# A fused sandwich layer on one core: y kept in the projection's bank, small operations moved to GpSimd, every engine's order rewritten

## What is computed

```
n   = layernorm(x)
o   = causal_conv(n, K) + D_vec * n          # K[d,t] = C[d] * sigmoid(A[d])**t * B[d], per channel
z   = n + gelu(o) @ W_proj.T + b_proj
y   = layernorm(z) * gamma + beta
t   = x + layernorm(y)
m   = layernorm(t); m_prev = m shifted by one token
r   = sigmoid((mu_r*m + (1-mu_r)*m_prev) @ W_r.T)
k   = relu((mu_k*m + (1-mu_k)*m_prev) @ W_k.T)**2
out = t + layernorm(r * (k @ W_v.T))
```

## Time and profile before

| | before |
|---|---|
| median of three runs | 176.42 us (175.55 to 176.43) |
| the profiled execution | 176.38 us |
| its span, first to last instruction | 174.7 us |
| PE matmul busy | 139.6 us (80% of the span), 913 matmuls |
| DVE busy | 146.9 us (84%), 433 instructions |
| ACT busy | 141.4 us (81%), 423 instructions |
| POOL busy | 130.5 us (75%), 149 instructions |
| mean granted TensorE clock | 0.962 of full speed |

### The profile page before, as it was taken

How to read it: one execution, slowest core, us unless ns; L and a number is a source line. 1 busy time by engine, 2 the same in 40 slices (tenths; PEclk the granted TensorE clock), 3 DMA queues, 4 the chain that set the end, 5 groups by cost and what they waited for, 6 DMA issues and landing times.

```text
span 174.7 us, 3232 instructions
## 1 busy us (share of the span) xinstructions
PE 139.6 (80%) x913; PEld 116.4 (67%) x913; DVE 146.9 (84%) x433; ACT 141.4 (81%) x423; POOL 130.5 (75%) x149
## 2 busy tenths in 40 slices
PE   0177556599997899799899999999998989899600
PEld 0065455599687796697687687987796769577600
DVE  0968899967899999999999999999999999933610
ACT  4456985768879989699799599799969997998960
POOL 4357478406996987576889989965989995897794
PEclk9999999669999999999999999999999999999975
DMA  4699500000000000000000100201100101405115
GB/s 114 161 274 338 165 0 2 4 0 0 0 0 2 4 0 4 0 4 0 0 0 4 60 4 0 64 0 60 60 4 13 49 7 55 126 9 171 60 60 180
DMA packets 18673, 8.98 MB, mean 51 GB/s; under 512 B 1504, under 2 KB 18656, under 8 KB 18656
## 3 DMA queue, kind: packets, MB, share of 16 engines
q1 hardware_dynamic: 18224, 8.79, 17.3%
q10 hardware_dynamic: 432, 0.00, 0.1%
HBM read 4.59 MB, written 4.19 MB: 50 GB/s over the span
## 4 chain that ended last, share of the span: by engine, by line
DVE 50%; PE 30%; issue 7%; POOL 6%; ACT 4%; ACTq 1%; POOLq 1%; DVEq 0%
DVE x_all L450 11%; DVE y L433 7%; DVE y_raw L383 4%; DVE t_raw L383 4%; DVE conv_scaled L418 4%; PE ps_v L634 4%; PE ps_prefix L580 4%; DVE conv L424 4%; PE ps_k L613 3%; PE ps_k L614 3%; DVE f L466 3%; PE ps_r L625 3%; PE ps_r L624 3%; PE ps_z L595 3%; DVE x_raw L383 2%
## 5 line engine op out<-in xcount | busy, mean ns | idle before, releaser
L279 ACT ACTIVATE xn<-x_all,x_bias,x_r 128x128 f32<-128x128 f32 x64 | 25.9, 494 | 3.4 <-POOL x_bias L187 3.0
L335 ACT ACTIVATE f_normal<-f,out_bias,f_r 128x128 f32<-128x128 f32 x64 | 26.2, 488 | 2.7 <-POOL out_bias L235 2.7
L595 PE MATMUL ps_z<-pv_T,gelu 128*128 128x128 f32 x128 | 23.8, 289 | 3.3 <-DVE y L433 1.6
L450 DVE SCALAR_TENSOR_TENSOR x_all<-y,y_r,x_all 128x128 f32<-128x128 f32 x64 | 25.8, 470 | 0.0
L624 PE MATMUL ps_r<-mixed_T,tsT 128*128 128x128 f32 x128 | 24.8, 276 | 0.8 <-ACT tanh L329 0.8
L211 POOL TENSOR_TENSOR y<-y,beta_row 128x512 f32<-128x512 f32 x16 | 20.4, 1275 | 6.4 <-DVE y L433 6.4
L625 PE MATMUL ps_r<-mixed_T,tsT 128*128 128x128 f32 x128 | 24.7, 275 | 0.0
L595 PEld LDWEIGHTS ps_z<-pv_T,gelu 128*128 128x128 f32 x128 | 20.4, 200 | 5.8 <-issue 4.0
L580 PE MATMUL ps_prefix<-prefix_ones,xn_pow 128*128 128x256 f32 x64 | 21.3, 417 | 2.1 <-DVE conv_scaled L418 2.0
L194 POOL TENSOR_TENSOR xn_pow<-xn,pow_token 128x512 f32<-128x512 f32 x16 | 20.4, 1278 | 1.8 <-ACT xn L279 1.8
L307 ACT ACTIVATE t_scaled<-x_all,t_r 128x128 f32<-128x128 f32 x64 | 20.3, 393 | 1.5 <-POOL t_r L223 1.4
(11 more groups left out here) (85 smaller groups left out, 358.7 us busy)
## 6 DMA issues: line engine op xcount, KB each, us to landing
out_x<-x_all SPq DMA_DIRECT2D x16, 256.0 KB, 2.2
x_all<-in_x SPq DMA_DIRECT2D x7, 512.0 KB, 5.9
x_all<-in_x SPq DMA_DIRECT2D x2, 256.0 KB, 3.6
w_pv<-in_W_proj SPq DMA_DIRECT2D x1, 64.0 KB, 4.6
w_pv<-in_W_v SPq DMA_DIRECT2D x1, 64.0 KB, 4.7
w_rk<-in_W_r SPq DMA_DIRECT2D x1, 64.0 KB, 5.0
w_rk<-in_W_k SPq DMA_DIRECT2D x1, 64.0 KB, 3.5
gamma_row<-in_gamma SPq DMA_DIRECT2D x1, 64.0 KB, 3.0
```

Source lines behind the costliest of these rows:

```text
L279: last = a_.activation(tile(xn[u % D], j), xa(u, j), ACT.Identity, bias=col(x_bias, u, j), scale=col(x_r, u, j))
L335: last = a_.activation(tile(f_normal[u % D], j), tile(f[u % D], j), ACT.Identity, bias=col(out_bias, u, j), scale=col(f_r, u, j))
L450: last = v_.scalar_tensor_tensor(xa(u, j), tile(y[u % D], j), col(y_r, u, j), xa(u, j), ALU.mult, ALU.add)
L595: t_.matmul(tile(ps_z[u % 2], j), tile(gelu[u % D], j), pv_T[:, 0, :], start=True, stop=False)
```

## The change

- **y stays in the bank.** `scale_z` and `add_beta` go. A new `gamma_z` [DVE] multiplies the whole bank by gamma in place (one 128x512 instruction, it waits for `square_z`); the new `scale_z` [DVE] does z * z_r + beta in place, four tiles. Statistics and residual read the bank. The SBUF ring `y` is gone. `project(u)` now waits for `residual(u - 2)` in place of `scale_z(u - 2)`.
- **Small operations.** The five 128x4 DVE instructions per unit (L443, L444, L459, L475, L476) go. Variance plus eps is now a POOL `tensor_scalar` ahead of each power, for one unit or a pair; the minus sign of the means is avoided by a negated W_v, a subtraction in out_bias and one in `add_f`. `keep_pv` becomes two instructions.
- **Statistics of x.** `POOLED` is 12: POOL takes the powers for units 4 to 11 too, in four pairs; `x_rsqrt` remains for units 12 to 15.
- **t of odd units.** `scale_t_pool` scales t on POOL for units 1, 3, 5, 7, 9, 11 and 13; ACT keeps the other nine.
- **Orders.** The four lists are rewritten.

```diff
-    POOLED = 4
+    POOLED = 12
+T_ON_POOL = (1, 3, 5, 7, 9, 11, 13)
...
-            def add_beta(u):
-                if u == 0:
-                    pool.wait_ge(s_rows, 16 * 2)
-                pool.wait_ge(y_scaled, u + 1)
-                yv = y[u % D][:].rearrange("p (j c) -> p j c", c=P)
-                g_.tensor_tensor(yv, yv, beta_row[:, None, :].to_broadcast([P, TILES, P]), ALU.add).then_inc(y_ready, 1)
-
             def y_scale_of(u, n):
-                pool.wait_ge(y_moments, u + n)
+                pool.wait_ge(y_stats, u + n)
+                g_.tensor_scalar(cols(y_ve, u, n), cols(y_raw, u, n)[:, :, 2], 1.0 / P, EPS, ALU.mult,
+                                 ALU.add).then_inc(y_ve_done, n)
+                pool.wait_ge(y_ve_done, u + n)
                 g_.tensor_tensor(cols(y_r, u, n), cols(y_ve, u, n), neg_half[:, 0:n * TILES],
                                  ALU.pow).then_inc(y_scale, n)
...
+            def scale_t_pool(u):
+                pool.wait_ge(t_scale, u + 1)
+                after(pool, tT_ready, u - D + 1)
+                for j in range(TILES):
+                    last = g_.tensor_scalar(tile(t_scaled[u % D], j), xa(u, j), col(t_r, u, j), 1.0, ALU.mult, ALU.mult)
+                last.then_inc(ts_pool_ready, 1)
...
-            def scale_z(u):
+            def gamma_z(u):
+
                 if u == 0:
                     dve.wait_ge(s_rows, 16 * 2)
+                dve.wait_ge(z_squares, u + 1)
+                z = ps_z[u % 2][:].rearrange("p (j c) -> p j c", c=P)
+                v_.tensor_tensor(z, z, gamma_row[:, None, :].to_broadcast([P, TILES, P]), ALU.mult).then_inc(z_gamma, 1)
+
+            def scale_z(u):
+
                 dve.wait_ge(z_scale, u + 1)
-                after(dve, t_ready, u - D + 1)
-                for j in range(TILES):
-                    last = v_.scalar_tensor_tensor(tile(y[u % D], j), tile(ps_z[u % 2], j), col(z_r, u, j),
-                                                   gamma_row[:], ALU.mult, ALU.mult)
-                last.then_inc(y_scaled, 1)
...
+                dve.wait_ge(z_gamma, u + 1)
+                for j in range(TILES):
+                    last = v_.scalar_tensor_tensor(tile(ps_z[u % 2], j), tile(ps_z[u % 2], j), col(z_r, u, j),
+                                                   beta_row[:], ALU.mult, ALU.add)
+                last.then_inc(y_ready, 1)
...
             def residual(u):
                 dve.wait_ge(y_scale, u + 1)
                 for j in range(TILES):
-                    last = v_.scalar_tensor_tensor(xa(u, j), tile(y[u % D], j), col(y_r, u, j), xa(u, j),
+                    last = v_.scalar_tensor_tensor(xa(u, j), tile(ps_z[u % 2], j), col(y_r, u, j), xa(u, j),
                                                    ALU.mult, ALU.add)
                 last.then_inc(t_ready, 1)
...
             def project(u):
...
-                after(pe, y_scaled, u - 1)
+                after(pe, t_ready, u - 1)
```

```diff
-            x_stats(2); x_pooled(2, 2); x_stats(4); convolve(0); x_stats(5); keep_pv(); x_stats(6); x_rsqrt(4, 4)
-            convolve(1); scale_z(0); x_stats(8); x_stats(9); y_moments_of(0); convolve(2); x_stats(10); residual(0)
...
+            x_stats(2); x_pooled(2, 2); x_stats(4); convolve(0); x_pooled(4, 2); keep_pv(); x_stats(6)
+            x_pooled(6, 2); convolve(1); x_stats(8); x_pooled(8, 2); gamma_z(0); convolve(2); x_stats(10)
+            scale_z(0); gamma_z(1); y_stats_of(0); scale_z(1); convolve(3); y_stats_of(1); residual(0)
...
+            convolve(5); scale_z(2); scale_z(3); y_stats_of(2); y_stats_of(3); x_stats(12); convolve(6); x_stats(13)
...
```

The new PE list around the projections, with what stands between them:

```diff
+            prefix_sum(11); keys(5)
+            values(3); transpose_xn(12); gates(5); transpose_t(6); prefix_sum(12); transpose_t(7); keys(6)
+            values(4); project(10); project(11); transpose_xn(13); prefix_sum(13); keys(7); values(5)
...
+            prefix_sum(15); gates(9); values(9); keys(10); gates(10); project(14); transpose_t(11); project(15)
+            values(10); keys(11); transpose_t(12); gates(11); keys(12); values(11); transpose_t(13); gates(12)
+            keys(13); values(12); transpose_t(14); gates(13); values(13); transpose_t(15); keys(14); gates(14)
+            keys(15); values(14); gates(15); values(15)
```

More of the change, by code:

```diff
@@ L245, in _ @@
[L245 to L249, removed]
@@ new lines, in _ @@
+            x_rsqrt(12, 4); scale_z(4); scale_z(5); y_stats_of(4); y_stats_of(5); convolve(8); gate(0); residual(4)
+            residual(5); t_stats_of(4); t_stats_of(5); f_stats_of(0); gate(1); gamma_z(6); convolve(9); gamma_z(7)
+            scale_z(6); scale_z(7); y_stats_of(6); y_stats_of(7); convolve(10); f_stats_of(1); residual(6)
+            residual(7); t_stats_of(6); t_stats_of(7); gate(2); gamma_z(8); f_stats_of(2); gamma_z(9); convolve(11)
+            scale_z(8); y_stats_of(8); scale_z(9); y_stats_of(9); gate(3); convolve(12); residual(8); residual(9)
@@ new lines, in _ @@
+            t_stats_of(8); t_stats_of(9); gate(4); gamma_z(10); f_stats_of(3); convolve(13); gamma_z(11)
+            scale_z(10); scale_z(11); y_stats_of(10); y_stats_of(11); gate(5); f_stats_of(4); f_stats_of(5)
+            residual(10); residual(11); t_stats_of(10); t_stats_of(11); gate(6); f_stats_of(6); gamma_z(12); gate(7)
+            gamma_z(13); convolve(14); scale_z(12); f_stats_of(7); y_stats_of(12); scale_z(13); y_stats_of(13)
+            gate(8); f_stats_of(8); convolve(15); residual(12); gate(9); f_stats_of(9); t_stats_of(12); residual(13)
@@ L537, in _ @@
+            t_stats_of(13); gamma_z(14); gate(10); scale_z(14); y_stats_of(14); f_stats_of(10); gamma_z(15)
+            scale_z(15); y_stats_of(15); residual(14); t_stats_of(14); residual(15); t_stats_of(15); gate(11)
+            f_stats_of(11); gate(12); f_stats_of(12); gate(13); f_stats_of(13); gate(14); f_stats_of(14); gate(15)
+            f_stats_of(15)
         @block.tensor
@@ L600, in transpose_t @@
             def transpose_t(u):
-                pe.wait_ge(ts_ready, u + 1)
+                if u in T_ON_POOL:
+                    pe.wait_ge(ts_pool_ready, T_ON_POOL.index(u) + 1)
+                else:
+                    pe.wait_ge(ts_ready, u + 1 - sum(v < u for v in T_ON_POOL))
                 after(pe, tT_copied, u)
@@ L635, in values @@
                 last.then_inc(v_ready, 1)
-            transpose_xn(0); centre_bias(); prefix_sum(0); transpose_pv(); transpose_rk(); transpose_xn(1)
-            project(0); prefix_sum(1); transpose_xn(2); prefix_sum(2); project(1); transpose_xn(3); prefix_sum(3)
-            transpose_xn(4); prefix_sum(4); project(2); transpose_xn(5); prefix_sum(5); transpose_t(0); project(3)
-            transpose_xn(6); mix_weights(); prefix_sum(6); keys(0); project(4); prefix_sum(7); transpose_xn(7)
-            project(5); gates(0); prefix_sum(8); transpose_xn(8); values(0); project(6); project(7); transpose_t(1)
@@ L642, in _ @@
-            transpose_xn(9); prefix_sum(9); gates(1); keys(1); transpose_xn(10); prefix_sum(10); project(8)
-            prefix_sum(11); transpose_t(2); transpose_xn(11); project(9); gates(2); transpose_t(3); transpose_xn(12)
-            keys(2); prefix_sum(12); gates(3); keys(3); values(1); transpose_t(4); project(10); project(11)
-            transpose_xn(13); prefix_sum(13); gates(4); keys(4); values(2); transpose_t(5); project(12); keys(5)
-            transpose_t(6); values(3); project(13); transpose_xn(14); gates(5); keys(6); gates(6); transpose_t(7)
@@ L647, in _ @@
-            prefix_sum(14); gates(7); transpose_t(8); keys(7); transpose_xn(15); values(4); transpose_t(9)
-            project(14); prefix_sum(15); keys(8); values(5); gates(8); keys(9); project(15); transpose_t(10)
-            values(6); gates(9); transpose_t(11); keys(10); values(7); gates(10); keys(11); values(8)
-            transpose_t(12); gates(11); values(9); keys(12); transpose_t(13); values(10); gates(12); transpose_t(14)
-            values(11); keys(13); values(12); gates(13); keys(14); transpose_t(15); values(13); gates(14); keys(15)
@@ L652, in _ @@
-            values(14); gates(15); values(15)
+            transpose_xn(0); centre_bias(); prefix_sum(0); transpose_pv(); transpose_xn(1); prefix_sum(1)
+            project(0); transpose_rk(); transpose_xn(2); prefix_sum(2); project(1); transpose_xn(3); prefix_sum(3)
+            mix_weights(); prefix_sum(4); transpose_xn(4); project(2); project(3); transpose_xn(5); prefix_sum(5)
+            transpose_t(0); prefix_sum(6); transpose_xn(6); keys(0); gates(0); transpose_xn(7); prefix_sum(7)
+            transpose_t(1); project(4); project(5); keys(1); prefix_sum(8); transpose_xn(8); values(0)
@@ new lines, in _ @@
+            transpose_t(2); gates(1); transpose_t(3); keys(2); gates(2); prefix_sum(9); transpose_xn(9); values(1)
+            project(6); project(7); gates(3); keys(3); transpose_xn(10); transpose_t(4); values(2); prefix_sum(10)
```

(8 more changed lines are left out.)

166 lines of the change are left out of this document (74 added, 92 removed).

## The result

The changed kernel takes **164.19 us** (median, 164.04 to 164.25) against 176.02 us for the kernel before beside it: a ratio of 0.9327, interval 0.9295 to 0.9359, so 6.7% faster. The forecast was 167.0 us, range 161.5 to 175.

A forecast was written before the change was run, and what follows sets the result against it. All engines were taken as nearly level, with PE's work unchanged and about 19 us of its losses partly recoverable. Start -4, low clock -2, middle -3 and tail -0.4 gave -9.4 from 176.38 us: 167.0 us, range 161.5 to 175.

The forecast's parts named there:

- the case: Whole kernel: the main forecast, faster at 162 to 170.5 us, chance 0.58.
- (a) Start: Start: x_rsqrt no longer before convolve(1) and a shorter residual(0), against gamma_z and longer bank hold; 4 us off.
- (b) low clock: Early part: PE denser from 20 to 30 us, so 2 of 3.3 us lost to the low clock return.
- (c) Middle: 60 to 160 us: DVE has a seventh of its time free, so 3 of PE's 4.8 idle us return.
- (d) Tail: Tail: the last two 128x4 instructions give way to one on POOL; 0.4 us off.
- the account of PE's losses: Up to 160 us: PE loses 10.9 + 3.3 + 4.8 = 19 us; the change returns only part and trims the tail.
- half of DVE's relief passes: Whole kernel: the terms together, -9.4 us, are about half of DVE's 19 us of relief.
- DVE's 128 us: DVE busy time over the whole kernel: -20 - 8.2 - 1.5 + 10.4 = -19 us, to 128.
- PE-bound in the middle: Rival, chance 0.10: PE 95% busy in the middle absorbs DVE's relief, only part of the start returns; 172 to 175 us.
- The bank's hold: Rival, chance 0.12: place and project wait for residual(u - 2), making the kernel slower; 178 to 184 us.
- The formula 73 + 6c: Kernel time if the bank sets the pace, c being the distance between pairs' projections; decides above c = 15.7.
- POOL in DVE's place: Rival, chance 0.15: POOL's 30 more small dependent steps cost each of seven pairs 1 us; 172 us, range 170.5 to 174.

The follow-up runs named there:

- e9: Changed kernel with POOLED = 4 again: x_rsqrt on DVE for units 4 to 11, the four x_scale pairs gone from POOL; 170.77 us.
- e8: Changed kernel with ten extra unused 128x512 additions on POOL ahead of add_f of units 0 to 9, outside the bank's cycle; ratio 0.9856 to the kernel before.
- e5: Kernel before in its old orders, only the small DVE operations moved to POOL (no minus signs, variance plus eps there); 174.51 us.
- e6: Changed kernel without gamma_z, so gamma is not applied; 162.1 us.
- e12: Changed kernel with x_rsqrt gone altogether: units 12 to 15 get their powers on POOL in two more pairs; 163.94 us.
- e7: Changed kernel with ten extra unused 128x512 additions on POOL between the wait for y's statistics and the power, in the bank's cycle; ratio 0.9963 to the kernel before.
- e2: Changed kernel with variance plus eps of y, t and f on DVE again, 48 small instructions; ratio 0.9844 to the kernel before.

## Why the prediction was right, and what it missed

**Right.** The direction, the case and the engine. Most of the signs that it named for the changed profile came, the 98% of PE in the middle among them; DVE's 131.9 us (125 to 131), ACT's 134.3 (131 to 134) and PE's idle 5.8 (6 or 7) lie just outside. The prices of the parts: gamma_z 0.69 us (0.68 taken), the residual out of the bank 17.5 us (17.6), ACT 134.3 us (132.5 plus), POOL 131.6 (133). The page's 120 against 58 cycles of the Trainium skill (VectorE: DVE Perf Modes, the TRN2 errata) did not show: statistics out of PSUM are 418 ns, those out of SBUF 419 to 421. The list laid out by hand put 12 to 17 us between projections and a start near 32 us; measured are 32.1 and 13.6 to 17.7.

**(a) Start, 4 us, and (b) low clock, 2 us.** As one sum they held: 5.1 us less idle to 60 us and 1.2 of clock. The 1.2 is half of the difference between PE's busy time at 1.2 GHz in the kernel before (first line) and in the changed one (second):

```profile
31.60:38.40 6.80, 5.86 (x24) 5.53 (x25) 5.07 (x14) 4.80 (x12) 1.01 (x1) 0.50 0.01 2
```

```profile
28.80:32.20 3.40, 3.40 (x13) 3.04 (x14) 3.37 (x11) 2.79 (x7) 2.74 (x6) 0.50 0.02 5
```

That the start is where much of the time is, e9 shows: its 7.7 us are complete at 54.90 us. The term was built from x_rsqrt's own length (1.9 and 2.8 us, 4.7 together). Undone, it costs 7.7: the 3.0 us of low clock, which came behind more idle time on PE, and 4.7. e8 has the same lists as the changed kernel up to there and was granted 1.00 from 10 to 40 us, where the changed kernel had 0.94:

```profile
10.00:40.00 30.00, 23.41 (x147) 20.19 (x148) 27.73 (x77) 24.92 (x81) 27.25 (x33) 1.00 0.33 97
```

Its projection of unit 2 starts 1.0 us earlier (31.11), that of unit 4 at 47.26, the same. After the change the slow stretch costs nothing that can be seen: the four timed executions took 164.04 and 164.20 us at a mean clock of 0.967 and 164.25 and 164.17 at 0.984 and 0.985. DVE sets the pace there. In e9's stretch from 43.6 us, where PE's matmuls are on the chain that ended last, it cost 3.0. What it cost before was not tried. The executions of the kernel before beside these runs point to 1 or 2 us: the three at 0.985 or 0.986 took 173.4 to 174.0, those at 0.957 to 0.967 took 174.1 to 176.5, but one at 0.982 took 175.9.

**(c) Middle, 3 us:** 3.2 measured. **(d) Tail, 0.4:** 0.4.

**What failed: the size, 9.4 us where 11.8 came (12.4 between the two profiled spans).** The step is the account of PE's losses, 19 us of idle time and slow clock. It took the rest of PE's busy time for work that stays. PE did the same 913 matmuls in 3.7 us less of busy time, and 1.2 of that is the clock. Most of the other 2.5 goes with PE's stops: in the records its row of overlapping matmuls is broken 22 times before and 12 times after. In a projection a matmul lasts 275 ns but the next starts 0.11 us behind it, so the last one ahead of a stop shows 0.16 us more of busy time, and the first one behind a stop lasts about 348 ns, 0.07 more. Ten stops fewer are an estimate of 2.3 us. The mean of 289 ns on the projection's first line before, 277 after, has the same two sources: eight of its matmuls ran at 1.2 GHz (421 ns), none as long after, and eight others lasted 347 to 377 ns, three after. So a stop costs more than its idle time, and the forecast priced only the idle time.

The sentence that half of DVE's relief passes has no support either: e5 passed 1.4 of 13.1 us, e6 1.4 of 11.9, e12 none, and in e9 3.7 us more of DVE cost 7.2.

**DVE's 128 us:** 131.9 came. The small operations on x were taken as 1.5 us less and are some 2.3 more. The remaining x_rsqrt was not seen as exposed: its operations have two SBUF inputs and ran beside POOL's. The three of L420 lasted 936 ns in the mean, where those of the same shape had 175 before; two of them took over 1.2 us:

```profile
53.57 1.28 DVE L420 SCALAR_TENSOR_TENSOR x_sq<-x_sq,x_v 128x16 f32<-128x16 f32 x1
...
53.55 1.27 POOL L194 TENSOR_TENSOR xn_pow<-xn,pow_token 128x512 f32<-128x512 f32 x1
```

**Scaling on POOL:** 0.37 us each, 0.30 taken, inside the bounds.

**The rivals.** PE-bound in the middle fits the old orders (e5) and was no ground for a small gain: 5.1 us of the idle time lay ahead of the middle, and 3.2 of the middle's 4.8 came back too. The bank's hold did not decide: no wait at a projection in the changed kernel, and the distance c was 15.4 us in the mean (32.1 to 124.4 in six pairs), under the 15.7 from which it was to count. e7 shows the mechanism: unit 14's projection came 5.4 us later, 0.9 us a pair for 1.04 us of delay. The formula 73 + 6c holds for the changed kernel (165.3 for 164.0) and falls short for e7 (c = 16.35, so 171.1 for 174.0), since it takes what comes behind the last pair as fixed, and e7 lost 4.6 us there. POOL in DVE's place was under-rated for the end: e8 puts it there as the next bound. Its sum was wrong too: seven pairs at 1 us each are 7, so 174 and not 172.

**What stays open.** The experiments don't add up to the gain: what was undone one at a time in the new orders cost 9.1 us (e2), 7.2 (e9) and 3.0 (e1), more than the 11.8 of the whole, while the small operations moved in the old orders brought 1.4. The parts and the orders need each other, and how much of the gain is y in the bank was not measured.

## What to carry to other kernels

Relief on the busiest engine is worth what its place in time makes of it: find the stretch in which the engine that must do all the work still idles, and take operations off the chain that feeds it there. Every stop that goes gives back more than its idle time. Moving small operations between engines pays only with the order written for it; the same move brought 0.8% in the old lists and its (smaller) undoing cost 5% in the new ones. To see where a variant loses, compare the start of one recurring instruction per unit, not the totals, and only between kernels whose lists for that engine are the same.

## What the runs showed that was not expected

Stalls of DVE beside POOL don't vanish with the instructions that suffered them: with 80 small ones gone, the residual from SBUF went from 470 to 559 ns in the mean (e5). With y read from PSUM no residual lasted above 352 ns. And the changed kernel and e8, with the same lists up to there, were granted 0.94 and 1.00 of TensorE's clock from 10 to 40 us, and their projections of unit 4 start at 47.25 and 47.26 us, while in e9 a low stretch on PE's chain cost 3.0 us.
